# A decoder layer on one Trainium2 core: sums over tokens taken by GpSimd additions and one matmul, or by matmuls over four token tiles

## The chip, the cores and the metric

The kernel runs on one core of one Trainium2 chip, as one launch. The metric is the device time of the launch in microseconds (us), lower is better; the median of three runs is given with the lowest and the highest. Engines: TensorE (matmuls, PE in the profile, PEld its weight loads), VectorE (DVE), ScalarE (ACT), GpSimd (POOL) and SyncE (SP, which issues the DMAs here). Each engine works through its own queue in order and waits on semaphores that the others raise.

## The reference

16 batches of 512 tokens with 512 channels, fp32. Linear attention with 16 heads, then a cross attention over channels, then a mixture of experts with one expert of 8 per batch, each followed by a layer norm. Cut to what matters here:

```
x = layernorm(x + linear_attention(x))                 # x1
scores = einsum('bhdn,bhen->bhde', q, k) * scale       # q = x*wq + bq, k = ctx*wk + bk; sum over tokens n
x = layernorm(x + channel_attention(x, ctx))           # x2, global and local weights
top1 = argmax(einsum('bh,he->be', x.mean(axis=1), Wr) + br)   # the mean is over the 512 tokens
h = relu(x @ W1[top1] + b1[top1]); out = h @ W2[top1] + b2[top1]
x = layernorm(x + out)
```

Two sums over the 512 tokens of a batch stand in it: that of `x1` per channel, since the scores with q = x*wq + bq and the bias bk of the keys come apart into terms of which one is (sum of x1)*wq*bk, and that of `x2` per channel, for the router.

## The kernel before

`mixers` computes both attentions for all batches and stores `x2` in HBM; `experts` then does the experts, with products split into high and low parts. Tokens lie in four tiles of 128 (`TT = 4`), channels in four groups of 128 (`CC = XH = 4`).

`mixers` is a software pipeline over steps i = 0 to 18 (`staged`: three written out, steps 3 to 14 as a loop on each engine, four written out). In step i, batch a = i gets its keys, values and queries, b = i - 1 its denominator, projection and first layer norm, c = i - 2 its channel attention and second norm, e = i - 3 its router. So from step 3 to step 15 all four are there; step 16 has b, c and e, step 17 c and e, step 18 e alone. The order in each engine's queue is written out by hand.

TensorE's queue in a step: the k product of a (three fp32r matmuls for each of four channel groups, L868), the denominators of b (L918), v of a, the broadcast of the reciprocals (L933, L940) around q of a, then the two sums over tokens: `mean_ps` of e (L949) and `sx_ps` of c (L956), then k of a's group 1, the router's product (L968), v and q, k and v of group 2, two tiles of the projection, the transposes of the channel weights (L990), q of group 2, the channel attention's output (L1011), the rest of the projection, k, v, q of group 3, and last the sum of the context (L1030) and the raw scores (L1043) of b, which use `x1`.

For the sums, GpSimd adds the four token tiles of `x1` (b, `tile_sum(0, ...)`) and of `x2` (c, `tile_sum(1, ...)`) at the end of its step into `x_sum` (L292, L296), three instructions on 128x512 each. A step later TensorE multiplies each 128 channels of `x_sum` with a column block of ones (32 columns): four products for each sum, which the profile shows as eight instructions, since an fp32 product is two. ScalarE copies the results out as `m_col` (L451, for the router) and `s_x` (L458), in this order and after both sums, because they lie in one PSUM bank. Behind them in ScalarE's queue stands `y_hi` of channel groups 2 and 3 (L405), from which GpSimd makes `y_lo` (L308) and after it adds a bias to all of `x_tok` in one instruction on 128x2048 (L312).

VectorE's queue in a step: the inner score products (L646, L647), the denominator (L778 and on), keys and values of group 0 (L536, L547, two scans), `y` times its reciprocal (L763), the outer score products (L653, L657), query and numerator (L558, L566, L576), then `token_sums` (L622, L623, L626), which reads `s_x`, the rest of the scores up to their scaled maximum (L667 to L682), keys and values of group 1 and so on. At the end of the step stand `xT_lo` of the next batch (L749) and L558, L566, L576 of group 3.

GpSimd's addition of `const_b` to `x1` (L331) waits for its own `x1` sum (`xsum_done`), and VectorE's write of `x2` (L595) for that of the batch before (`x2sum_done`).

Of the kernel before, what the change touches and what calls it, by code (L numbers as in the profile page):

```python
# [11 lines left out]
P = 128  # L12
# [43 lines left out]
def mixers(nc, d, idx, x2_dram, x2_stored):  # L56

    with ExitStack() as ctx:
        def sb(name, shape, dt=F32):
            return ctx.enter_context(nc.sbuf_tensor(name, shape, dt))  # L60

        def sem(name):
            return ctx.enter_context(nc.semaphore(name))
# [57 lines left out]
        k_all, k_all2 = sb("k_all", [P, XH]), sb("k_all2", [P, XH])  # L121
        aT = sb("aT", [P, XH, P])
        const_b = sb("const_b", [P, C])
        x_sum = sb("x_sum", [P, 2, C])
        m_col = sb("m_col", [P, CC])
        logits = sb("logits", [1, NE])
        top = sb("top", [1, NE])
# [50 lines left out]
        mean_mm, mcol_done, route_mm, logit_done, top_done, idx_done = (  # L178
            sem(n) for n in ("mean_mm", "mcol_done", "route_mm", "logit_done", "top_done", "idx_done"))
        found_done = sem("found_done")  # L180
        xsum_done, x2sum_done = sem("xsum_done"), sem("x2sum_done")
        rall_done = sem("rall_done")

        block = ctx.enter_context(nc.Block())
# [55 lines left out]
        def _(pool):  # L240
# [41 lines left out]
                    pool.wait_ge(mr_done[n], due)  # L282
                pool.tensor_tensor(shift[:, n, :], m_r[:, n, :], minus[:, :], ALU.mult).then_inc(shift_done[n], 1)

            def tile_sum(n, b, x, x_done, used, done):

                if (due := upto(b, TT, TT)) is not None:
                    pool.wait_ge(x_done, due)

                if (due := upto(b - 1, 1, 1)) is not None:  # L290
                    pool.wait_ge(used, due)
                pool.tensor_tensor(x_sum[:, n, :], x[:, 0, :], x[:, 1, :], ALU.add).then_inc(done, 1)  # L292
                for t in range(2, TT):
                    if (due := upto(b, TT - 1, t - 1)) is not None:
                        pool.wait_ge(done, due)
                    pool.tensor_tensor(x_sum[:, n, :], x_sum[:, n, :], x[:, t, :], ALU.add).then_inc(done, 1)  # L296

            def step(i):
                b, c = i - 1, i - 2
                if inside(b):  # L300
# [13 lines left out]
                if inside(c):  # L314

                    if (due := upto(c, 1, 1)) is not None:
                        pool.wait_ge(kall2_done, due)

                    if (due := upto(c, 1, 1)) is not None:
                        pool.wait_ge(c_mm, due)  # L320
                    pool.tensor_tensor(diag[:, :, :], ident[:, :].unsqueeze(1).broadcast_to([P, XH, P]),
                                       k_all2[:, :].unsqueeze(2).broadcast_to([P, XH, P]), ALU.mult).then_inc(diag2_done, 1)
                    if (due := upto(c, 1, 1)) is not None:
                        pool.wait_ge(kb_done, due)

                    if (due := upto(c, 1, 1)) is not None:
                        pool.wait_ge(g_mm, due)
                    if (due := upto(c, TT - 1, TT - 1)) is not None:
                        pool.wait_ge(xsum_done, due)
                    for t in range(TT):  # L330
                        pool.tensor_tensor(x1[:, t, :], x1[:, t, :], const_b[:, :], ALU.add).then_inc(x1c_done, 1)  # L331
                if inside(b):
# [8 lines left out]
                    rstd_of(0, b)  # L341
                if inside(c):
                    rstd_of(1, c)
                if inside(b):
                    tile_sum(0, b, x1, x1_done, sx_mm, xsum_done)
                if inside(c):
                    tile_sum(1, c, x2, x2_done, mean_mm, x2sum_done)

            staged(pool, step)

# [164 lines left out]
        def _(dve):  # L515
# [62 lines left out]
            def residual(n, b, t):  # L578
                mm, res, done, src, dst = ((proj_mm, x_tok, res1_done, x_tok, x_tok),
                                           (out_mm, x1, res2_done, x1, x2))[n]  # L580
                if (due := upto(b, TT, t + 1)) is not None:
                    dve.wait_ge(mm, due)
                if n == 0:
                    if (due := upto(b, 1, 1)) is not None:
                        dve.wait_ge(xb_done, due)
                else:
                    if (due := upto(b, TT, t + 1)) is not None:
                        dve.wait_ge(x1c_done, due)

                    if (due := upto(b - 1, TT - 1, TT - 1)) is not None:  # L590
                        dve.wait_ge(x2sum_done, due)
                    if (due := upto(b - 1, 16, 16)) is not None:
                        dve.wait_ge(x2_stored, due)
                ps = WIDE[t % 2]
                dve.tensor_tensor(dst[:, t, :], ps[:, :], src[:, t, :], ALU.add).then_inc(done, 1)  # L595
# [265 lines left out]
        def _(pe):  # L861
# [34 lines left out]
            def step(i):  # L896
# [46 lines left out]
                        pe.wait_ge(den_max, due)  # L943
                if inside(e):

                    if (due := upto(e, TT - 1, TT - 1)) is not None:
                        pe.wait_ge(x2sum_done, due)
                    for j in range(CC):
                        last = pe.matmul(mean_ps[:, j, :], x_sum[:, 1, j * P:j * P + P], ones[:, 0:SUM], start=True, stop=True)  # L949
                    last.then_inc(mean_mm, 1)  # L950
                if inside(c):

                    if (due := upto(c, TT - 1, TT - 1)) is not None:
                        pe.wait_ge(xsum_done, due)
                    for h in range(XH):
                        last = pe.matmul(sx_ps[:, h, :], x_sum[:, 0, h * P:h * P + P], ones[:, 0:SUM], start=True, stop=True)  # L956
                    last.then_inc(sx_mm, 1)
                if inside(a):
                    qkv(a, 1, "k")
# [496 lines left out]
```

## Time and profile before

| | |
|---|---|
| runs | median 2728.85 us (2728.75 to 2729.05, 3 runs) |
| the profiled execution, its span | 2728.0 us |
| TensorE busy | 2471.1 us (91%) |
| VectorE busy | 1893.2 us (69%) |
| ScalarE busy | 994.4 us (36%) |
| GpSimd busy | 684.0 us (25%) |
| DMA | 97 GB/s in the mean, 264.09 MB |

The profile's own execution took its span and less than 1 us around it. `mixers` takes the first 1262 us of it, `experts` the rest. The page cuts the span into 40 slices of 68 us; in each row a digit is the busy share in tenths:

```profile
PE   7988888888889888854999999999999999999998
DVE  6899999999999999964455555555555455545553
POOL 3344444444454445442011001100111011101110
```

The reader sees two parts: in the first eighteen slices VectorE is at nine tenths and TensorE at eight, in the others TensorE alone is full. Times in rows are us from the start of the span; a row of the timeline has start, length, engine, line, operation, output<-inputs, shapes (partitions x elements) and number of instructions, and in brackets for how long the engine was idle before it and who ended that.

### The profile page before, as it was taken

The page shows a single profiled execution, that of the slowest core. Times are in us where ns is not written, and L with a number is a line of the kernel's source. Part 1 is how long each engine was busy: PE and PEld are TensorE (multiplying, and loading weights), DVE is VectorE, ACT ScalarE, POOL GpSimd, SP SyncE. Part 2 cuts the span into 40 slices and gives each one's busy share as a digit, 9 for nine tenths or more (in the row PEclk, how much of TensorE's full clock was granted, in tenths as well). Part 3 has the DMA queues.
Part 4 walks back from the last instruction along what each step waited for, and adds up shares of the span by engine and source line. Part 5 has one row for each costly group of instructions (what it writes and reads, how often), then busy time and mean ns, then how long its engine had stood idle before and what let it go on. Part 6 is the DMA issues. An engine that isn't in the chain of part 4 may idle for free.

```text
span 2728.0 us, 35480 instructions
## 1 busy us (share of the span) xinstructions
PE 2471.1 (91%) x11584; PEld 2008.6 (74%) x11584; DVE 1893.2 (69%) x2904; ACT 994.4 (36%) x1639; POOL 684.0 (25%) x521
## 2 busy tenths in 40 slices
PE   7988888888889888854999999999999999999998
PEld 5766666667667666743888887878878788888886
DVE  6899999999999999964455555555555455545553
ACT  4433433344434434322333333333333333333332
POOL 3344444444454445442011001100111011101110
PEclk9999999999999999976999999999999999999999
DMA  4121112112222221113333343324332433243321
GB/s 189 47 78 57 42 71 77 69 70 77 77 77 77 77 77 38 44 74 125 107 129 111 101 143 128 119 87 143 130 122 82 143 135 123 76 143 135 135 72 68
DMA packets 59002, 264.09 MB, mean 97 GB/s; under 512 B 9106, under 2 KB 9106, under 8 KB 43922
## 3 DMA queue, kind: packets, MB, share of 16 engines
q1 hardware_dynamic: 58898, 262.60, 26.8%
q8 instruction: 78, 1.28, 0.2%
q14 instruction: 26, 0.21, 0.0%
HBM read 229.02 MB, written 33.55 MB: 96 GB/s over the span
## 4 chain that ended last, share of the span: by engine, by line
PE 52%; issue 0%; DVE 0%; DMA 0%; ACT 0%; POOL 0%; ACTq 0%; POOLq 0%; DVEq 0%
PE h_ps L1358 26%; PE acc L1376 26%; PE t_ps L1336 1%; DMA x_res<-x_scratch 0%; DVE we_lo L1257 0%; ACT x_res L1242 0%; DVE stats_e L1310 0%; ACT x2T_hi L1213 0%; POOL rstd_f L1186 0%; ACT we_hi L1205 0%; ACTq L1056 0%; DVE x2T_lo L1264 0%; DVE mv_e L1321 0%; POOLq L1056 0%; POOL var_f L1183 0%
## 5 line engine op out<-in xcount | busy, mean ns | idle before, releaser
L1229 ACT ACTIVATE hid<-h_ps,b 128x512 f32<-128x512 f32 x256 | 176.1, 688 | 727.3 <-PE h_ps L1358 727.3
L1280 DVE CAST h_hi<-hid 128x512 fp32r<-128x512 f32 x256 | 113.5, 443 | 457.3 <-ACT hid L1229 457.3
L868 PE MATMUL bank<-xT_hi,w_hi 128*128 128x512 f32 x768 | 332.2, 433 | 106.1 <-DVE kv_sum L547 79.6
L1358 PE MATMUL h_ps<-x2T_hi,we_hi 128*128 128x512 f32 x1024 | 407.1, 398 | 15.6 <-issue 9.8
L1358 PE MATMUL h_ps<-x2T_lo,we_hi 128*128 128x512 f32 x1024 | 400.5, 391 | 0.0
L1358 PE MATMUL h_ps<-x2T_hi,we_lo 128*128 128x512 f32 x1024 | 400.5, 391 | 0.0
L1376 PE MATMUL acc<-we_hi,h_lo 128*128 128x512 f32 x1024 | 399.0, 390 | 0.0
L1376 PE MATMUL acc<-we_hi,h_hi 128*128 128x512 f32 x1024 | 398.8, 389 | 0.0
L1376 PE MATMUL acc<-we_lo,h_hi 128*128 128x512 f32 x1024 | 398.8, 389 | 0.0
L1257 DVE TENSOR_TENSOR we_lo<-raw,we_hi 128x1024 fp32r<-128x1024 f32 x256 | 314.6, 1230 | 107.4 <-ACT we_hi L1205 107.4
L1183 POOL TENSOR_TENSOR var_f<-mv_e,ln_eps_e 128x4 f32<-128x4 f32 x16 | 17.3, 1082 | 1328.1 <-DVE mv_e L1321 1328.1
L868 PE MATMUL bank<-xT_lo,w_hi 128*128 128x512 f32 x768 | 318.0, 414 | 0.0
L868 PE MATMUL bank<-xT_hi,w_lo 128*128 128x512 f32 x768 | 318.0, 414 | 0.0
L1205 ACT ACTIVATE we_hi<-raw 128x1024 fp32r<-128x1024 f32 x256 | 269.5, 1054 | 118.1 <-DMA raw<-in_w 118.1
L868 PEld LDWEIGHTS bank<-xT_hi,w_hi 128*128 128x128 f32 x768 | 153.5, 200 | 156.1 <-DVE kv_sum L547 86.2
L1283 DVE TENSOR_TENSOR h_lo<-hid,h_hi 128x512 fp32r<-128x512 f32 x256 | 237.8, 929 | 8.8
L1358 PEld LDWEIGHTS h_ps<-x2T_hi,we_hi 128*128 128x128 f32 x1024 | 193.1, 189 | 50.5 <-issue 12.2
L1358 PEld LDWEIGHTS h_ps<-x2T_lo,we_hi 128*128 128x128 f32 x1024 | 193.3, 189 | 44.9 <-issue 6.9
L1358 PEld LDWEIGHTS h_ps<-x2T_hi,we_lo 128*128 128x128 f32 x1024 | 193.0, 189 | 41.6
L1376 PEld LDWEIGHTS acc<-we_hi,h_hi 128*128 128x128 f32 x1024 | 192.4, 188 | 40.0
L1376 PEld LDWEIGHTS acc<-we_lo,h_hi 128*128 128x128 f32 x1024 | 192.3, 188 | 39.7
L1376 PEld LDWEIGHTS acc<-we_hi,h_lo 128*128 128x128 f32 x1024 | 192.3, 188 | 39.7
(147 smaller groups left out, 3968.3 us busy)
## 6 DMA issues: line engine op xcount, KB each, us to landing
raw<-in_w SPq DMA_DIRECT2D x256, 512.0 KB, 3.3
xT_raw<-in_xT SPq DMA_DIRECT2D x16, 1024.0 KB, 9.5
x_tok<-in_x_tok SPq DMA_DIRECT2D x16, 1024.0 KB, 6.7
ctx_tok<-in_ctx_tok SPq DMA_DIRECT2D x16, 1024.0 KB, 8.8
ctx_T<-in_ctxT SPq DMA_DIRECT2D x16, 1024.0 KB, 4.7
x_scratch<-x SPq DMA_DIRECT2D x16, 1024.0 KB, 4.8
x_res<-x_scratch SPq DMA_DIRECT2D x16, 1024.0 KB, 4.9
out_dram<-x_res SPq DMA_DIRECT2D x16, 1024.0 KB, 4.8
```

The costliest lines, as they stand in the source:

```text
L868: last = pe.matmul(out, lhsT, rhs, start=(n == 0), stop=(n == 3 * len(pairs) - 1))
L1183: pool.tensor_tensor(var_e[:, :], mv[:, :, 1], ln_eps[:, :], ALU.add).then_inc(ve_done, 1)
L1205: act.activation(w_hi[:, f % NW, :], raw[:, f % NR, :], ACT.Copy).then_inc(whi_done, 1)
L1229: act.activation(hid[:, f % 2, :], h_ps[f % 2][:, :], ACT.Relu, bias=b1[:, parity, f:f + 1]).then_inc(h_done, 1)
L1257: dve.tensor_tensor(w_lo[:, f % NW, :], raw[:, f % NR, :], w_hi[:, f % NW, :].bitcast(F32), ALU.subtract).then_inc(wlo_done, 1)
L1280: dve.tensor_copy(h_hi[:, s, :], hid[:, f % 2, :]).then_inc(hhi_done, 1)
L1283: dve.tensor_tensor(h_lo[:, s, :], hid[:, f % 2, :], h_hi[:, s, :].bitcast(F32), ALU.subtract).then_inc(hlo_done, 1)
L1336: last = pe.transpose(t_ps[j % 2][:, t * P:t * P + P], x_res[parity][:, t, j * P:j * P + P], ident[:, :])
L1358: last = pe.matmul(h_ps[f % 2][:, :], wx[:, s, js], xx[parity][:, j, :], start=(n == 0), stop=(n == 3 * CC - 1))
L1376: last = pe.matmul(acc[t][:, :], hx[:, s, ts], wx[:, sw, C:], start=(f == 0 and n == 0), stop=(f == FC - 1 and n == 2))
```

## The change

The additions on GpSimd, the buffer `x_sum` and the semaphores `xsum_done` and `x2sum_done` go. TensorE multiplies each of the four token tiles of `x1` and `x2` itself with the ones and lets PSUM accumulate them: 16 products for each sum where there were 4, so 64 instructions for 16 in a step that has both. It waits for the normalised tiles (`x1_done`, `x2_done`). GpSimd's L331 now waits for `sx_mm`, VectorE's L595 for `mean_mm`.

```diff
@@ mixers, GpSimd
-                    if (due := upto(c, TT - 1, TT - 1)) is not None:
-                        pool.wait_ge(xsum_done, due)
+                    if (due := upto(c, 1, 1)) is not None:
+                        pool.wait_ge(sx_mm, due)
                     for t in range(TT):
                         pool.tensor_tensor(x1[:, t, :], x1[:, t, :], const_b[:, :], ALU.add).then_inc(x1c_done, 1)
...
-                if inside(b):
-                    tile_sum(0, b, x1, x1_done, sx_mm, xsum_done)
-                if inside(c):
-                    tile_sum(1, c, x2, x2_done, mean_mm, x2sum_done)
@@ mixers, VectorE
-                    if (due := upto(b - 1, TT - 1, TT - 1)) is not None:
-                        dve.wait_ge(x2sum_done, due)
+                    if (due := upto(b - 1, 1, 1)) is not None:
+                        dve.wait_ge(mean_mm, due)
@@ mixers, TensorE
-                    if (due := upto(e, TT - 1, TT - 1)) is not None:
-                        pe.wait_ge(x2sum_done, due)
+                    if (due := upto(e, TT, TT)) is not None:
+                        pe.wait_ge(x2_done, due)
                     for j in range(CC):
-                        last = pe.matmul(mean_ps[:, j, :], x_sum[:, 1, j * P:j * P + P], ones[:, 0:SUM], start=True, stop=True)
+                        for t in range(TT):
+                            last = pe.matmul(mean_ps[:, j, :], x2[:, t, j * P:j * P + P], ones[:, 0:SUM],
+                                             start=(t == 0), stop=(t == TT - 1))
                     last.then_inc(mean_mm, 1)
                 if inside(c):
 
-                    if (due := upto(c, TT - 1, TT - 1)) is not None:
-                        pe.wait_ge(xsum_done, due)
+                    if (due := upto(c, TT, TT)) is not None:
+                        pe.wait_ge(x1_done, due)
                     for h in range(XH):
-                        last = pe.matmul(sx_ps[:, h, :], x_sum[:, 0, h * P:h * P + P], ones[:, 0:SUM], start=True, stop=True)
+                        for t in range(TT):
+                            last = pe.matmul(sx_ps[:, h, :], x1[:, t, h * P:h * P + P], ones[:, 0:SUM],
+                                             start=(t == 0), stop=(t == TT - 1))
                     last.then_inc(sx_mm, 1)
```

## Rows read from the trace of the kernel before

**Rows 1.** Stretch, us, busy of PE, PEld, DVE, ACT, POOL (count), PEclk, DMA, GB/s.
```profile
191.80:1087.90 896.10, 765.94 (x3889) 609.96 (x3889) 836.57 (x1405) 360.92 (x745) 416.50 (x301) 0.95 0.18 70
```
**Rows 2.** Timeline of TensorE: one looped step, then parts of later steps.
```profile
640.15 2.43 PE L918 MATMUL bank<-qk,head_sum 128*32 128x128 f32 x32 [0.42 <-DVE qk L566]
...
645.18 0.40 PE L868 MATMUL bank<-xT_hi,w_lo 128*128 128x512 f32 x1
...
652.74 0.98 PE L949 MATMUL bank<-ones,x_sum 128*128 128x32 f32 x8
653.55 1.06 PE L956 MATMUL bank<-ones,x_sum 128*128 128x32 f32 x8
654.45 0.48 PE L868 MATMUL bank<-xT_hi,w_hi 128*128 128x512 f32 x1
...
670.77 0.80 PE L868 MATMUL bank<-xT_hi,w_hi 128*128 128x512 f32 x1 [4.40 <-DVE kv_sum L547]
...
711.34 0.49 PE L868 MATMUL bank<-xT_hi,w_hi 128*128 128x512 f32 x1 [0.70 <-DVE xT_lo L749]
...
725.88 0.97 PE L949 MATMUL bank<-ones,x_sum 128*128 128x32 f32 x8
...
1084.54 0.47 PE L868 MATMUL bank<-xT_hi,w_hi 128*128 128x512 f32 x1 [0.56 <-issue]
```
**Rows 3.** Timeline of ScalarE in the same step.
```profile
654.90 0.17 ACT L458 ACTIVATE s_x<-bank 128x4 f32<-128x4 f32 x1
```
**Rows 4.** Timeline of VectorE in the same step.
```profile
643.80 0.28 DVE L778 TENSOR_SCALAR den<-bank 128x128 f32<-128x128 f32 x1
...
646.42 0.75 DVE L547 SCALAR_TENSOR_TENSOR kv_sum<-bank,b_qkv,k_sum 128x512 f32<-128x512 f32 x1
...
660.40 4.57 DVE L622 TENSOR_TENSOR s_q<-s_x,cols 128x4 f32<-128x4 f32 x1
...
668.88 0.29 DVE L682 TENSOR_SCALAR neg_scaled<-neg_max 128x4 f32<-128x4 f32 x2
...
675.64 0.69 DVE L558 SCALAR_TENSOR_TENSOR q<-e_q,r_q 128x512 f32<-128x512 f32 x1
...
707.40 3.70 DVE L749 TENSOR_TENSOR xT_lo<-xT_raw,xT_hi 128x1024 fp32r<-128x1024 f32 x2 [0.82 <-ACT xT_hi L382]
711.02 1.77 DVE L558 SCALAR_TENSOR_TENSOR q<-e_q,r_q 128x512 f32<-128x512 f32 x1
```
**Rows 5.** Timeline of VectorE in step 16.
```profile
1172.68 0.15 DVE L622 TENSOR_TENSOR s_q<-s_x,cols 128x4 f32<-128x4 f32 x1
...
1183.22 0.28 DVE L682 TENSOR_SCALAR neg_scaled<-neg_max 128x4 f32<-128x4 f32 x2
```
**Rows 6.** Timeline of GpSimd in the looped step.
```profile
659.89 5.05 POOL L312 TENSOR_TENSOR x_tok<-x_tok,rows 128x2048 f32<-128x2048 f32 x1
...
707.88 4.36 POOL L296 TENSOR_TENSOR x_sum<-x_sum,x 128x512 f32<-128x512 f32 x2
```
**Rows 7.** Timeline of TensorE in steps 16, 17 and 18.
```profile
1167.65 1.75 PE L949 MATMUL bank<-ones,x_sum 128*128 128x32 f32 x8
1169.21 1.90 PE L956 MATMUL bank<-ones,x_sum 128*128 128x32 f32 x8
...
1221.66 1.58 PE L949 MATMUL bank<-ones,x_sum 128*128 128x32 f32 x8 [1.77 <-POOL x_sum L296]
...
1259.06 1.91 PE L949 MATMUL bank<-ones,x_sum 128*128 128x32 f32 x8 [12.87 <-POOL x_sum L296]
```
**Rows 8.** Short stretches in steps 16 and 17, columns as in rows 1.
```profile
1167.50:1170.80 3.30, 3.30 (x17) 3.21 (x16) 3.30 (x3) 0.17 (x1) 2.91 (x2) 0.50 0.01 5
1171.70:1175.40 3.70, 0.25 (x8) 0.13 (x6) 3.63 (x6) 1.23 (x2) 2.50 (x3) 0.50 0.01 2
1213.70:1218.00 4.30, 4.29 (x20) 4.29 (x21) 0.00 (x0) 2.78 (x4) 4.11 (x4) 0.50 0.17 72
1218.00:1219.90 1.90, 1.89 (x14) 1.69 (x13) 0.00 (x0) 0.00 (x0) 1.82 (x2) 0.83 0.94 388
```

More of the change, by code:

```diff
@@ L123, in mixers @@
         const_b = sb("const_b", [P, C])
-        x_sum = sb("x_sum", [P, 2, C])
         m_col = sb("m_col", [P, CC])
@@ L180, in mixers @@
         found_done = sem("found_done")
-        xsum_done, x2sum_done = sem("xsum_done"), sem("x2sum_done")
         rall_done = sem("rall_done")
@@ L283, in rstd_of @@
                 pool.tensor_tensor(shift[:, n, :], m_r[:, n, :], minus[:, :], ALU.mult).then_inc(shift_done[n], 1)
[L285 to L296, printed above, removed]
             def step(i):
```

## The prediction

> **What bounds the kernel now.** I read the engines' busy times over the twelve looped steps of the mixer first, then one step of it on TensorE, ScalarE, VectorE and GpSimd in order of time, and last the granted clock. The twelve steps last 896.1 us, so one lasts 74.7 us; VectorE is busy for 836.57 us of them (93%), TensorE for 765.94 (85%), GpSimd for 416.50 (46%) [rows 1]. So a step goes at VectorE's pace, with TensorE close behind: TensorE waits 4.40 us for VectorE's `kv_sum` of L547 before its product at 670.77 and 0.70 us for `xT_lo` at 711.34 [rows 2]. Work added to TensorE ahead of the 4.40 us wait could vanish in it. The question is who waits for the sums themselves. ScalarE reads them out (L458) at 654.90 [rows 3]; VectorE comes to that result only at 660.40, at L622, 5.3 us after it is there [rows 4]. That slack of 5.3 us is what the added work has to fit into.
>
> The same VectorE rows hold the other side. L622 is an operation on 128x4 and takes 4.57 us there, and 0.15 us at 1172.68 [rows 4, 5]; meanwhile GpSimd runs its one 128x2048 addition of 5.05 us [rows 6]. A 128x512 operation with two SBUF operands (L558) takes 0.69 us at 675.64 and 1.77 us at 711.02, where GpSimd is in the `x_sum` additions of L296, 4.36 us for two [rows 4, 6]. So an operation of VectorE that meets one of GpSimd waits until that one ends. Taking the sums from GpSimd gives VectorE time back.
>
> The expert part (from about 1262 us on) has none of the changed lines and I cost it at nothing.
>
> **GpSimd's additions leave.** Each is three instructions per batch. In a looped step they lie beside the end of VectorE's step: the two `xT_lo` at 707.40 and the three operations L558, L566 and L576 behind them. One of the three costs 1.77 - 0.69 = 1.08 us too much [rows 4], so the three 3.2 us, besides what `xT_lo` gains. But that is not what the step gains. Next late is TensorE's den product (L918), for which VectorE's L778 waits. It now ends at 640.15 + 2.43 = 642.58 and L778 starts at 643.80 [rows 2, 4]. TensorE itself gets earlier only by its two waits on VectorE: 0.42 us before L918, and of the 0.70 us before the first product 0.14 us, since the entry into a step costs 0.56 us even where nothing is waited for (1084.54) [rows 2]. So den ends at 642.02, and L778 gains 1.8 us, not 3.2. Then L547 needs the v product, which ends at 645.18 + 0.40 - 0.56 = 645.02: L547 starts there instead of at 646.42, and 1.4 us are left of the gain [rows 2, 4]. Beyond this the old queue order holds: GpSimd's `const_b` addition, `y_lo` and the 128x2048 addition stay and go on meeting VectorE.
>
> **TensorE's sums grow.** 16 matmul instructions per step (each fp32 product is two) become 64. At full clock 16 take 654.45 - 652.74 = 1.71 us, 0.107 us each [rows 2]. At half clock eight take 1169.21 - 1167.65 = 1.56 us, 0.195 each, and the next eight 1.90 us [rows 7], 0.24 each; I take 0.20, near the start to start value, since the 1.90 hold the end of the last one too. So 64 take 6.8 us at 2.4 GHz and 12.8 us at 1.2 GHz.
>
> Which clock? From 1167.50 to 1170.80 TensorE did nothing but these sums, busy all 3.30 us, at a granted clock of 0.50, and at 1171.70 to 1175.40 it is still 0.50. From 1213.70 to 1218.00 it did the products of L1043 at 0.50, and from 1218.00 on the row's mean is 0.83, so it had risen [rows 8]. So the sums did not lift the clock and the products of L1043 did. I take from it that the sums do not hold it either, and that it falls during the 6.8 us. No row shows that directly; today's sums last 1.7 us. I put the fall in the middle: 32 at 0.107 and 32 at 0.20 make 9.8 us. Bounds: after a quarter of them 1.7 + 9.6 = 11.3 us, after three quarters 5.1 + 3.2 = 8.3 us.
>
> **One looped step.** Where the clock did not fall before them, the sums start at 725.88, that is 651.2 in the step I use. Their start hangs on VectorE's `y` (L763), so it moves with VectorE, to 651.2 - 1.4 = 649.8. They end 9.8 us later, at 659.6. From their end to the `s_x` result are 654.90 + 0.17 - 654.45 = 0.62 us [rows 2, 3], so L622 can start at 660.2. VectorE would be there at 660.40 - 1.4 - 2 x 1.0 = 657.0 (L566 and L576 ahead of L622 are free of `y_lo`, which now comes later, because ScalarE has the copies L451 and L458 ahead of `y_hi` of chunks 2 and 3 in its queue, and GpSimd takes `y_lo` from there). So VectorE waits 3.2 us for the sums: a new wait, and behind it in VectorE's queue stand the score operations, on which ScalarE's exponentials wait. The relief from the 128x2048 addition doesn't come either: `y_lo` and it are held up by the same wait and now meet the operations behind L622. A row shows that alignment: in step 16 L622 starts at 1172.68 and L682 ends at 1183.50, 10.8 us [rows 5]. So L682 ends at 660.2 + 10.8 = 671.0, against 668.88 + 0.29 = 669.17 now [rows 4]: 1.9 us later per step. Bounds from 8.3 and 11.3 us of sums: 0.4 to 3.4 us. TensorE's own 8.1 us more (9.8 for 1.7) meet a start 2.9 us earlier than 652.74 and the wait of 4.40 us at 670.77, and VectorE's `kv_sum`, 1.9 us later, still comes last there, so nothing is added for TensorE. Thirteen steps (3 to 15) have both sums with all the rest: 13 x 1.9 = 24.7 us, bounds 5 and 44. Step 2 has one sum only, 32 instructions or 1.7 us more inside 5.3 us of slack: nothing.
>
> **The last three steps**, without attention products, where TensorE is cold. Step 16: 48 more at 0.20 are 9.6 us, less the 1.2 us by which VectorE comes later than `s_x` today (sums end 1169.21 + 1.90, L622 starts 1172.68, 0.4 us lie between) and 1.0 us of relief ahead: 7.4 us. Step 17: today TensorE idles 1.77 us for GpSimd at 1221.66 [rows 7]; that goes, the first 16 or so run in it at full clock (1.5 us saved), 9.6 - 1.8 - 1.5 = 6.3 us. Step 18: the GpSimd additions of 4 us ahead of 1259.06 go, 24 more at 0.20 come: 0.8 us. Sum 14.5 us, bounds 8 (step 16 warm) and 17.
>
> **Sum.** 2728.0 + 24.7 + 14.5 = 2767.2 us span. The runs' median is 2728.85, 0.8 us more than the profiled span, so 2768 us.
>
> **Two rules of the skill.** The Trainium skill, SBUF — State Buffer, "SBUF: two separate sides", says that GpSimd and VectorE share one port pair as an exclusive lock and that the loser is blocked for the whole instruction. The rows of 4.57 us agree. Taken alone it speaks for a gain, which is rival B. The Trainium skill, TensorE: Matmul & The Clock Gate, "What's actually happening", says that activity releases the throttle; if weight loads and short matmuls back to back are activity, the clock holds: rival A.
>
> **The rivals.** The forecast: the clock falls within the sums and VectorE waits for them. Chance 0.66.
> A: the clock holds in the loop. For it: the sums keep TensorE busy without a gap, and in the rows at 725.88 they run at 0.107. Against it: the 3.30 us at 0.50. Sums of 6.8 us end at 656.6, L622 at 657.3, L682 ends at 668.1: 1.1 us per step gained, 13 x 1.1 = 14 us, against 14.5 us lost at the end: 2729 us. Chance 0.15.
> B, the other side: the clock holds and GpSimd's 128x2048 addition meets the reductions of L678 (a single operand, 1.3 us for two) in place of two-operand work. Then 1.1 + 1.2 = 2.3 us per step are gained, 30 us, less 14.5: 2713 us. It decides itself at L622: the sums must be read before VectorE gets there. Chance 0.10.
> C: the clock falls early and stays at half through the products behind the sums. Eleven of these take 645.18 - 642.58 = 2.6 us at full clock, so 24 at half clock cost up to 5.7 us more; with 9.6 us of added sums (11.3 for 1.7) that is 15.3 us, less the 2.9 and 4.40 us of before and 2.8 us that the twelve products at 670.77 gain if the clock is up there: TensorE becomes the bound, by about 5 us per step, 65 + 17 = 82: 2811 us. For it: nothing in the sums lifts the clock. Chance 0.09.
>
> **How the numbers follow.** Range: A lies at its lower end, the forecast's upper bound (44 + 17) at 2790; 2727 to 2790 leaves out B and C, 0.19. About 0.2%, 5.5 us, is what a measurement of this kernel can tell from no change. Faster: B, 0.10. Same: A, 0.15, and a thin edge of the forecast, 0.01. Slower: the rest, 0.74.
>
> **What would show it.** Right: the granted clock falls to 0.50 within the 64 sums (L949 and L956 now); VectorE idle before L622, released by ScalarE's `s_x`; L558, L566, L576 at the end of a step at 0.69 us; no wait at `xT_lo` before the first product; a step of 76 to 77 us; L622 in step 16 about 7 us later against its step's start. Wrong: a granted clock of 1.00 throughout the sums (A), a step below 74 us (B), or the longest wait of TensorE gone and VectorE waiting for products of L868 (C).

## The result, and the profile after

The kernel with TensorE's sums takes 2743.45 us in the median (2740.08 to 2748.45, four runs), the kernel before in the same comparison 2728.8 us (2728.09 to 2729.05, four runs). The ratio is 1.0059, 95% interval 1.0044 to 1.0073: 0.6% slower. 2768 us was forecast, so the direction was right, the range (2727 to 2790) holds the time, and the loss was forecast at 2.7 times its size. The profiled execution is the fastest of the four, 2740.08 us, with a span of 2738.3 us; all accounts below go from span to span, 2728.0 to 2738.3, which is 10.3 us. The medians are 14.7 us apart; the other 4.3 us are the distance of the fastest run of the kernel after from its median, and only the fastest was profiled.

The page of the kernel after, engines' busy time, share and instructions:

```profile
span 2738.3 us, 36806 instructions
PE 2588.5 (95%) x12352; PEld 2128.4 (78%) x12352; DVE 1829.8 (67%) x2904; ACT 993.5 (36%) x1639; POOL 527.3 (19%) x425
```

TensorE has 768 instructions and 117 us of busy time more, VectorE 63 us less although it executes the same instructions, GpSimd 157 us less. The twelve looped steps, with the columns of [rows 1]:

```profile
194.60:1096.60 902.00, 854.98 (x4464) 700.22 (x4464) 782.07 (x1405) 360.06 (x744) 294.62 (x228) 0.93 0.18 70
```

A step lasts 75.2 us where it lasted 74.7. VectorE falls from 836.57 to 782.07 us of work, which is 4.5 us per step, and the step is still longer: its time is now in waits. One looped step on TensorE, to set beside [rows 2] (its first product is the one at 636.91, not shown, without any idle time before it):

```profile
646.09 0.72 PE L914 MATMUL bank<-rden_all,head_all 128*128 128x512 f32 x2 [0.74 <-ACT rden_all L415]
...
650.09 3.65 PE L931 MATMUL bank<-ones,x 128*128 128x32 f32 x32
653.57 5.57 PE L940 MATMUL bank<-ones,x 128*128 128x32 f32 x32
658.96 0.77 PE L849 MATMUL bank<-xT_hi,w_hi 128*128 128x512 f32 x1
```

The first 32 instructions last 3.48 us from start to start (0.109 each), the next 32 5.39 us: the sums together 8.87 us. Stretches of the same time, with us, TensorE's busy time and count, granted clock, DMA share and GB/s, then the sums of step 16:

```profile
650.10:655.00 4.90, 4.90 (x46) 1.00 0.11 45
655.00:656.00 1.00, 1.00 (x8) 0.58 0.00 0
656.00:662.00 6.00, 6.00 (x22) 0.50 0.00 0
662.00:668.00 6.00, 6.00 (x33) 1.00 0.00 0
1171.20:1178.00 6.80, 6.80 (x34) 0.50 0.12 48
1178.00:1184.90 6.90, 6.88 (x33) 0.50 0.00 0
```

The clock falls from 2.4 to 1.2 GHz within the sums, after 46 of the 64 instructions, although TensorE is busy without a gap; it stays low behind them and is back at 662. In step 16 it was low before and the sums pass at half clock throughout, 13.8 us. VectorE and ScalarE in the looped step:

```profile
633.91 2.36 DVE L730 TENSOR_TENSOR xT_lo<-xT_raw,xT_hi 128x1024 fp32r<-128x1024 f32 x2 [0.82 <-ACT xT_hi L363]
636.19 0.69 DVE L539 SCALAR_TENSOR_TENSOR q<-e_q,r_q 128x512 f32<-128x512 f32 x1
...
642.50 0.29 DVE L759 TENSOR_SCALAR den<-bank 128x128 f32<-128x128 f32 x1 [1.90 <-PE bank L899]
...
659.64 0.17 DVE L603 TENSOR_TENSOR s_q<-s_x,cols 128x4 f32<-128x4 f32 x1 [2.27 <-ACT s_x L439]
...
660.11 2.37 DVE L648 TENSOR_TENSOR a_v<-rows,s_q 128x512 f32<-128x512 f32 x2
662.40 6.79 DVE L655 TENSOR_TENSOR s_a<-s_a,a_v 128x512 f32<-128x512 f32 x2
...
670.30 0.28 DVE L663 TENSOR_SCALAR neg_scaled<-neg_max 128x4 f32<-128x4 f32 x2
```

```profile
659.43 0.17 ACT L439 ACTIVATE s_x<-bank 128x4 f32<-128x4 f32 x1
```

```profile
663.59 5.05 POOL L297 TENSOR_TENSOR x_tok<-x_tok,rows 128x2048 f32<-128x2048 f32 x1
```

Against [rows 4]: the two `xT_lo` last 2.36 us where they lasted 3.70, and L539 (L558 before) 0.69 where it was 1.77, which is the relief. VectorE then waits 1.90 us for the denominators, and 2.27 us at L603 (L622 before), released by ScalarE's copy of the sums: the new wait. And L655 (L674 before) takes 6.79 us for two instructions, because GpSimd's 5.05 us addition [rows 6] now lies beside it and no more beside L622.

### The profile page after: what moved, and what is told of

The parts are those of the page before. It is cut to its first block, busy times and chain, and to the rows that moved or that the text cites. A ratio compares the mean times of both kernels' runs of the same rounds, so it can differ in the third digit from the quotient of the medians.

```text
span 2738.3 us, 36806 instructions
## 1 busy us (share of the span) xinstructions
PE 2588.5 (95%) x12352; PEld 2128.4 (78%) x12352; DVE 1829.8 (67%) x2904; ACT 993.5 (36%) x1639; POOL 527.3 (19%) x425
## 4 chain that ended last, share of the span: by engine, by line
PE 52%; DVE 0%; issue 0%; DMA 0%; ACT 0%; POOL 0%; ACTq 0%; POOLq 0%; DVEq 0%
PE h_ps L1343 26%; PE acc L1361 25%; PE t_ps L1321 1%; DMA x_res<-x_scratch 0%; DVE we_lo L1242 0%; ACT x_res L1227 0%; DVE stats_e L1295 0%; ACT x2T_hi L1198 0%; POOL rstd_f L1171 0%; ACT we_hi L1190 0%; ACTq L1041 0%; DVE x2T_lo L1249 0%; DVE mv_e L1306 0%; POOLq L1041 0%; POOL var_f L1168 0%
```

## Where the 10.3 us come from

I cut both traces at the same instructions: the first of the products that broadcast the reciprocals (L933 before, L914 after) in steps 3 and 16, the transposes of the channel weights in step 16, and the first product of the experts.

| stretch | before | after | difference | forecast |
|---|---|---|---|---|
| start to step 3 | 199.06 | 194.62 | -4.4 | 0 |
| steps 3 to 15 (13) | 965.83 | 974.09 | +8.3 | +24.7 |
| step 16 to the first expert product | 113.32 | 126.76 | +13.4 | +14.5 |
| `experts` | 1449.8 | 1442.9 | -6.9 | 0 |
| sum | 2728.0 | 2738.3 | +10.3 (rounded parts: 10.4) | +39.2 |

The last row of the table is a surprise: the change touches nothing in `experts`. TensorE's costliest group in that part, of the kernel before and of the kernel after (line, engine, operation, shapes and count, then busy us and mean ns, then the idle time before its instructions and by whom ended):

```profile
L1358 PE MATMUL h_ps<-x2T_hi,we_hi 128*128 128x512 f32 x1024 | 407.1, 398 | 15.6 <-issue 9.8 <-DVE we_lo L1257 5.8
```

```profile
L1343 PE MATMUL h_ps<-x2T_hi,we_hi 128*128 128x512 f32 x1024 | 406.6, 397 | 9.7 <-DVE we_lo L1242 5.8 <-issue 3.9
```

"issue" is time in which TensorE waited for nothing that the profile shows. It was 9.8 us and is 3.9 us. It stands at fixed places of the loop over the batches (one turn does two of them), two per turn before and one after:

```profile
1637.72 0.49 PE L1358 MATMUL h_ps<-x2T_hi,we_hi 128*128 128x512 f32 x1 [0.72 <-issue]
...
1640.91 0.39 PE L1358 MATMUL h_ps<-x2T_hi,we_hi 128*128 128x512 f32 x1 [1.55 <-issue]
```

```profile
1655.14 0.49 PE L1343 MATMUL h_ps<-x2T_hi,we_hi 128*128 128x512 f32 x1 [1.05 <-issue]
...
1834.17 0.49 PE L1343 MATMUL h_ps<-x2T_hi,we_hi 128*128 128x512 f32 x1 [0.68 <-issue]
```

## The experiments

The theory is the forecast's: relief of VectorE, sums in which the clock falls, a wait for them. Rivals: that relief and sums are worth something else than each was put at and meet by chance; that the loss is the order of the queues and not the clock; and, for `experts`, that the gain comes from some other state of the chip and not from the code. Times are medians, ratios against the kernel before in the same comparison, with 95% intervals.

**The relief alone.** GpSimd's additions are gone as in the change, TensorE does no more products than before.

```diff
@@ mixers, TensorE, against the kernel after; the other sum alike
-                        for t in range(TT):
-                            last = pe.matmul(sx_ps[:, h, :], x1[:, t, h * P:h * P + P], ones[:, 0:SUM],
-                                             start=(t == 0), stop=(t == TT - 1))
+                        last = pe.matmul(sx_ps[:, h, :], x1[:, 0, h * P:h * P + P], ones[:, 0:SUM], start=True, stop=True)
```

> Leaves out work: TensorE sums token tile 0 alone (4 products a sum, as in the kernel before), GpSimd adds nothing; so the two sums are those of a quarter of the tokens. It shows what GpSimd's additions cost alone. Theory (VectorE is freed of them, but TensorE's den product is next late): a looped step of 72.5 us (74.7 before), no wait of VectorE before its use of s_x, time 2690 to 2705. Rival (the whole 4.4 us of VectorE's time comes back): a step of 70.3 us, 2675. Rival (VectorE is not what sets the step): a step of 74.7 us, 2728.

Measured: 2692.7 us, ratio 0.9869 (0.9852 to 0.9885), a looped step 72.38 us. The relief is worth 2.29 us per step. This is inside what was expected, and VectorE has no wait at L603. L603 takes 4.56 us there, as before the change: beyond the two `xT_lo` and the operations behind them, GpSimd and VectorE go on meeting as the forecast said.

```profile
632.96 0.97 PE L930 MATMUL bank<-ones,x 128*128 128x32 f32 x8
633.77 1.06 PE L937 MATMUL bank<-ones,x 128*128 128x32 f32 x8
...
642.28 4.56 DVE L603 TENSOR_TENSOR s_q<-s_x,cols 128x4 f32<-128x4 f32 x1
```

**The sums alone.** GpSimd adds as before, each of TensorE's products for the sums is done four times.

```diff
@@ mixers, TensorE, against the kernel before; the other sum alike
                     for h in range(XH):
-                        last = pe.matmul(sx_ps[:, h, :], x_sum[:, 0, h * P:h * P + P], ones[:, 0:SUM], start=True, stop=True)
+                        for t in range(TT):
+                            last = pe.matmul(sx_ps[:, h, :], x_sum[:, 0, h * P:h * P + P], ones[:, 0:SUM], start=True, stop=True)
```

> The kernel before with its GpSimd additions, but TensorE does each product of the sums four times (same result). It shows the 64 instructions alone. Theory (the clock falls in the sums and VectorE waits for them): granted clock 0.50 from about 5 us into the sums, VectorE idle before L622 for 0.5 to 1.5 us, a looped step of 76.5 to 77.5 us, time 2760 to 2775. Rival (the sums fit into the slack of 5.3 us and TensorE's wait of 4.4 us): a step of 74.7 us and only the last three steps longer, 2740.

Measured: 2786.8 us, ratio 1.0214 (1.0194 to 1.0233), a looped step 77.62 us; both are above what was expected. The longer sums cost 2.95 us per step. The wait stands at the place that was named and is longer than the 0.5 to 1.5 us that were expected:

```profile
666.64 3.65 PE L950 MATMUL bank<-ones,x_sum 128*128 128x32 f32 x32
670.13 5.57 PE L958 MATMUL bank<-ones,x_sum 128*128 128x32 f32 x32
...
676.19 0.16 DVE L622 TENSOR_TENSOR s_q<-s_x,cols 128x4 f32<-128x4 f32 x1 [2.34 <-ACT s_x L458]
```

-2.29 and +2.95 make +0.66 us per step; the whole change measures +0.50 (75.17 less 74.67, the mean of twelve steps). The two parts nearly add up. So the small net loss is a difference of two large terms, 30 us and 38 us over thirteen steps.

**A wider product with the ones.** The same 64 instructions with the same weights, but 128 columns of ones in place of 32, so TensorE streams four times as much. The results need more of PSUM than is free in the old bank, so each sum goes to one of the two banks of the scores, with four more waits on three semaphores; `SUM` is the number of columns.

```diff
@@ against the kernel after
-SUM = 32
+SUM = 128
...
-        sx_ps, mean_ps = (DEN_BANK[:, n:n + XH * SUM].rearrange("p (h e) -> p h e", h=XH) for n in (P, P + XH * SUM))
+        sx_ps, mean_ps = (b[:, :].rearrange("p (h e) -> p h e", h=XH) for b in (G_BANK, C_BANK))
```

> The changed kernel with one size changed: the moving operand of the sums is 128 columns of ones instead of 32, with the same number of instructions and the same weights; the results go to the two banks of the scores, which are free then. Theory (the sums let the clock fall because they stream little): granted clock 1.00 through the sums of a looped step, which last 7.1 us instead of 9, VectorE waits 0.5 us instead of 2.3, a step of 73.5 us (75.2 in the changed kernel), and steps 16 to 18 shorter by 2 to 5 us: time 2715 to 2725. Rival (wider products cost more time than the clock gives): sums of 9 us or more, 2743 or above. Rival (the clock falls for another reason, the weight loads): clock 0.50 as before, 2743 to 2750.

Measured: 2706.07 us, ratio 0.9919 (0.9902 to 0.9935), a looped step 72.90 us, which is faster than was expected. The timeline around the sums, then their stretch (columns as above):

```profile
635.49 3.77 PE L935 MATMUL bank<-ones,x 128*128 128x128 f32 x32
639.10 3.74 PE L948 MATMUL bank<-ones,x 128*128 128x128 f32 x32
...
643.33 0.16 DVE L603 TENSOR_TENSOR s_q<-s_x,cols 128x4 f32<-128x4 f32 x1 [0.55 <-ACT s_x L439]
```

```profile
635.50:642.60 7.10, 7.10 (x66) 1.00 0.09 38
```

The granted clock is 1.00 from the first to the last, the sums last 7.11 us where they lasted 8.87, VectorE waits 0.55 us where it waited 2.27. The kernel does more work per sum and is 37 us faster than the one with 32 columns, faster even than the kernel before (8 us of that lie in `experts`, see below). The forecast's mechanism is seen here from its other side: the clock held, and the wait shrank with it. That it is the number of columns that lets the clock fall or holds it is the plain reading, but the banks and the four waits were changed with the columns, and no run puts 32 columns into the new banks, so this one step isn't shown apart from them. In step 16, where the clock is low as the sums begin, the 128 columns bring it up:

```profile
1141.50:1144.50 3.00, 3.00 (x15) 0.50 0.22 90
1144.50:1147.00 2.50, 2.50 (x21) 0.81 0.00 0
1147.00:1150.70 3.70, 3.70 (x34) 1.00 0.00 0
```

The 64 instructions there last 9.2 us (1141.54 to about 1150.7); those with 32 columns stayed at 0.50 for all of their 13.8 us.

**The router's sum moved back in the queue.** Nothing needs `mean_ps` soon, VectorE needs `sx_ps`. TensorE's sum for the router goes behind k of group 2, ScalarE's copy of it and the router's product behind that.

```diff
@@ mixers, TensorE, against the kernel after
-                if inside(e):
-
-                    if (due := upto(e, TT, TT)) is not None:
-                        pe.wait_ge(x2_done, due)
-                    for j in range(CC):
-                        for t in range(TT):
-                            last = pe.matmul(mean_ps[:, j, :], x2[:, t, j * P:j * P + P], ones[:, 0:SUM],
-                                             start=(t == 0), stop=(t == TT - 1))
-                    last.then_inc(mean_mm, 1)
...
+                    qkv(a, 2, "k")
                 if inside(e):
...
+                    for j in range(CC):
+                        for t in range(TT):
+                            last = pe.matmul(mean_ps[:, j, :], x2[:, t, j * P:j * P + P], ones[:, 0:SUM],
+                                             start=(t == 0), stop=(t == TT - 1))
+                    last.then_inc(mean_mm, 1)
```

> The changed kernel with the router's sum moved: TensorE does it behind the k product of group 2, where it waited 4.4 us in the kernel before, and the router's product and ScalarE's copy follow it; only the 32 instructions of the scores' sum stay where they were. Theory (VectorE's wait for s_x is what the change costs in a looped step): no wait of VectorE at s_x, a step of 72.5 to 73 us, steps 16 to 18 about 6 us longer than before instead of 13, time 2695 to 2712. Rival (TensorE's own added work is the bound): VectorE waits elsewhere for TensorE's products, a step of 75 us, 2735 to 2745.

Measured: 2690.17 us, ratio 0.9861 (0.9844 to 0.9877), a looped step 72.19 us: the fastest of all kernels here, together with the one below, and faster than was expected. In the step shown each sum alone passes at full clock:

```profile
632.16 3.65 PE L927 MATMUL bank<-ones,x 128*128 128x32 f32 x32
...
641.45 4.57 DVE L599 TENSOR_TENSOR s_q<-s_x,cols 128x4 f32<-128x4 f32 x1
...
646.93 3.65 PE L944 MATMUL bank<-ones,x 128*128 128x32 f32 x32
```

```profile
632.10:635.60 3.50, 3.50 (x33) 1.00 0.17 70
646.90:650.40 3.50, 3.50 (x33) 1.00 0.00 0
```

That isn't so in every step: of the thirteen sums for the scores in steps 3 to 15 three lasted 4.2 to 4.5 us, at a mean granted clock of 0.82 (487.40 to 491.70), 0.81 (921.00 to 925.30) and 0.76 (1064.60 to 1069.20). VectorE has no wait for `s_x` in any of the thirteen, and the step (72.19 us) is that of the relief alone (72.38 us): the sums have become free in the loop. They aren't free behind it: from step 16 to the first expert product it takes 116.7 us, 109.4 in the relief alone. The work is that of the change, only the order differs. The rival that it is the order is therefore right too, for a different part of the same wait: 64 instructions back to back are long at full clock (7.11 us with 128 columns), and they are slower still at half.

**Both of these.**

```diff
@@ against the kernel with the router's sum moved back
-SUM = 32
+SUM = 128
```

> The router's sum moved as in router_later, and the sums with 128 columns of ones as in cols128. Theory (two separate costs: VectorE's wait in the looped step, which the move alone removes, and cold sums in steps 16 to 18, which 128 columns shorten): looped step as router_later, 72.2 us, from the last broadcast of step 16 to the first expert product 2 to 5 us less than its 116.7 us, time 2684 to 2689. Rival (the bank of const_b, now written by the router's sum, makes a new wait): 2690 or more.

Measured: 2690.78 us, ratio 0.9862 (0.9846 to 0.9878), a looped step 72.05 us. No difference from the one above. From step 16 to the first expert product it takes 118.2 us against 116.7, which is not the shortening that was expected: a stall of TensorE with the releaser "issue", 2.62 us, stands before the sums of step 17.

**The scores' sum on TensorE, the router's with GpSimd.**

```diff
@@ mixers, TensorE, against the kernel before
-                    if (due := upto(c, TT - 1, TT - 1)) is not None:
-                        pe.wait_ge(xsum_done, due)
+                    if (due := upto(c, TT, TT)) is not None:
+                        pe.wait_ge(x1_done, due)
                     for h in range(XH):
-                        last = pe.matmul(sx_ps[:, h, :], x_sum[:, 0, h * P:h * P + P], ones[:, 0:SUM], start=True, stop=True)
+                        for t in range(TT):
+                            last = pe.matmul(sx_ps[:, h, :], x1[:, t, h * P:h * P + P], ones[:, 0:SUM],
+                                             start=(t == 0), stop=(t == TT - 1))
...
@@ mixers, GpSimd
-                if inside(b):
-                    tile_sum(0, b, x1, x1_done, sx_mm, xsum_done)
```

> One part of the change alone: the sum of x1 for the scores is accumulated by TensorE, that of x2 for the router stays with GpSimd's additions. 40 instructions of sums in a step, 4.3 us. Theory (VectorE's wait at s_x is the price, its meetings with GpSimd the gain): the sums end before VectorE comes, no wait at s_x, but x2's three additions still meet VectorE at the end of its step: 72.5 to 73.5 us a step, time 2705 to 2720. Rival (any accumulation on TensorE costs): 2730 or more.

Measured: 2694.24 us, ratio 0.9876 (0.9859 to 0.9892), a looped step 72.31 us, faster than was expected. With the additions of `x2` left on GpSimd the step keeps all of the relief (72.31 against 72.38): taking away those of `x1` is enough. The trace shows why those of `x2` cost nothing there. Without the others ahead of it VectorE is further on, and they lie beside its products of scores, which read a PSUM bank and go on at 0.68 us each, and beside its wait for the denominators; in the kernel before they reached into L566 and L576, 1.67 and 1.75 us each:

```profile
692.82 0.68 DVE L645 TENSOR_TENSOR a_v<-bank,cols 128x512 f32<-128x512 f32 x1
...
693.15 1.29 POOL L292 TENSOR_TENSOR x_sum<-x 128x512 f32<-128x512 f32 x1 [5.98 <-ACT x L391]
...
693.42 0.68 DVE L644 TENSOR_TENSOR s_a<-bank,cols 128x512 f32<-128x512 f32 x1
```

The opposite split, `x1` with GpSimd and `x2` on TensorE, was not run. The 40 instructions of both sums lasted 4.4 to 6.0 us in the looped steps, so here too the clock fell in some, and VectorE had no wait for `s_x` in any of them.

**Moving TensorE's code.** The change adds, by my count, 480 instructions to TensorE's program: the sums are written at ten places, each gets twelve more products, and a product is four instructions (the profile shows two loads and two matmuls for an fp32 product). The kernel before, with waits that are met at once put at the head of TensorE's program, moves the code of `experts` without touching it:

```diff
@@ mixers, TensorE, against the kernel before
         def _(pe):
+            for _ in range(480):
+                pe.wait_ge(xT_in, 16)
```

> The kernel before with 480 waits that are already met at the start of TensorE's queue, as many instructions as the change adds to TensorE's code. Nothing else differs, so it shows what the place of the expert loop's code costs. Theory (the second stall in each turn of TensorE's expert loop, 0.9 to 1.6 us with no releaser, comes from where its code lies): from the first expert product to the end 1443 us as in the changed kernel (1449.8 before), one such stall a turn in place of two; the start is 0 to 15 us later for the waits themselves. Rival (the shorter expert part comes from the state in which mixers leaves the engines): 1449.8 us and two stalls.

Measured: 2739.96 us, ratio 1.0041 (1.0027 to 1.0055); the waits themselves delay the start by 19 us. As was expected, from the first expert product (1297.41) to the end it takes 1443.0 us: the figure of the kernel after (1442.9), not that of before (1449.8). The same group as above:

```profile
L1360 PE MATMUL h_ps<-x2T_hi,we_hi 128*128 128x512 f32 x1024 | 406.6, 397 | 9.9 <-DVE we_lo L1259 5.8 <-issue 4.1
```

This was tried at other distances: 32 waits in the kernel after, then 32 and 224 in the kernel before, with the same edit.

> The changed kernel with 32 waits that are already met at the start of TensorE's queue: with the 480 instructions of the change that makes 512. Theory (place of the code, repeating every 128, 256 or 512 instructions): the second stall in a turn of the expert loop is back, 1449 to 1450 us from the first expert product to the end in place of 1442.9. Rival (state of the engines, or another period): 1443 us.

> The kernel before with 32 met waits at the start of TensorE's queue; only the place of its code changes. Theory (the two stalls in a turn of the expert loop hang on where its code lies, finer than 480 instructions): one stall a turn and 1443 us from the first expert product to the end. Rival (only a large shift matters): two stalls and 1449.8 us.

> As before_pad32 with 224 waits, which is 480 less 256. Theory (a period of 256 instructions or a divisor of it): as with 480 waits, one stall a turn and 1443 us. Rival (no period there): 1449.8 us.

Measured, with the time from the first expert product to the end:

| kernel | whole | first expert product | `experts` | "issue" in that group |
|---|---|---|---|---|
| before | 2728.8 | 1278.21 | 1449.8 | 9.8 |
| before, 32 waits (one run, before 2728.22) | 2745.68 | 1277.20 | 1466.7 | 19.4 |
| before, 224 waits (one run, before 2728.22) | 2724.14 | 1281.47 | 1440.9 | 2.5 |
| before, 480 waits | 2739.96 | 1297.41 | 1443.0 | 4.1 |
| after | 2743.45 | 1295.47 | 1442.9 | 3.9 |
| after, 32 waits | 2743.7 | 1303.44 | 1443.0 | 3.7 |

Places and "issue" are those of the profiled run, which for the kernel after with 32 waits is the slowest of its four, 2748.13 us; that kernel has a ratio of 1.0053 (1.0037 to 1.007). Only the runs with 480 and with 224 waits came out near what was expected; the two with 32 waits didn't (1466.7 where 1443 was expected, and 1443.0 where 1449 to 1450 was). With 32 waits in the kernel before each turn of the loop has one long stall:

```profile
1640.07 0.49 PE L1360 MATMUL h_ps<-x2T_hi,we_hi 128*128 128x512 f32 x1 [3.91 <-issue]
...
1823.85 0.79 PE L1360 MATMUL h_ps<-x2T_hi,we_hi 128*128 128x512 f32 x1 [3.83 <-issue]
```

So where TensorE's instructions of that loop lie makes 26 us of difference (1440.9 to 1466.7, single runs) without one instruction of the loop changed, and 32 instructions ahead of it, which cost nothing themselves, cost 17 us. 9.6 of these are longer "issue"; with them comes the clock, which is at half behind four of the five long stalls, as in the row here, and was at 1.00 at this place in the kernel before:

```profile
1642.00:1644.00 2.00, 2.00 (x6) 0.50 0.00 0
```

The idea behind the run of the kernel after with 32 waits, that the pattern repeats with 512 instructions so that 480 and 32 make a whole turn, fell: it stayed at 1443.0. The other kernels fit: the relief alone, with as many TensorE instructions as before, has 1449.8 us in `experts` like the kernel before (2691.5 - 1241.71); the sums alone, with the 480 more, 1442.0 (2783.0 - 1341.01). It matters for the ratios above: `experts` takes 1441.8 us with 128 columns, 1442.6 with the router's sum moved back and 1442.9 with the scores' sum alone on TensorE. So 7 to 8 us of what these kernels gain over the kernel before come from the place of the code and not from what was changed in `mixers`, and the relief alone is the fastest of all up to the first expert product (1241.71, against 1246.34 with the router's sum moved back and 1278.21 before).

## Why the prediction was right in its mechanism and wrong in its size

The mechanism came as forecast, the size didn't: 39.2 us were forecast and 10.3 came. The term that failed is the relief of VectorE. It put the start of the sums 1.4 us earlier; they start 2.3 us earlier, because the 0.56 us that the forecast left as the price of entering a step were a wait for `xT_lo` like the others and went too. `experts` at nothing (6.9 us) and the length of the sums (5.5 us) come next.

**Which resource it is about: right.** VectorE paces the step, and the sums are on the path through `s_x` and not through TensorE's time. The wait at L603 stands in each looped step, 1.4 to 4.2 us; 3.2 were forecast.

**The clock falls within the sums: right, and nearly at the place.** 46 of 64 instructions passed first in the step shown, where the middle was taken. The sums last 8.87 us there and 9.38 us in the mean of steps 3 to 15, for 9.8; the thirteen lie between 8.04 (step 3) and 10.80, all but the first within the bounds of 8.3 and 11.3. The middle was a choice between two bounds and read off no row, so that it came this close is in part luck. In the sum this is 0.42 us per step too much, 5.5 us in thirteen.

**The relief of VectorE: right in kind, too small in size.** This is the step that failed most. I let TensorE's first product gain 0.14 of its 0.70 us wait, because the entry into step 15 (the first one written out behind the loop) shows 0.56 us of "issue" [rows 2], and I took that for the price of any entry. It isn't one. In the kernel before, `xT_lo` of that step ends at 1080.74 + 3.70 = 1084.44, and the product starts at 1084.54:

```profile
1080.74 3.70 DVE L749 TENSOR_TENSOR xT_lo<-xT_raw,xT_hi 128x1024 fp32r<-128x1024 f32 x2 [0.81 <-ACT xT_hi L382]
```

By these rows the 0.56 us were a wait for VectorE's `xT_lo` that the profile gave no releaser, and this `xT_lo` was one of those that GpSimd stretched (3.70 us, 2.36 without it). The kernels that keep the additions of `x1` on GpSimd all show the 0.56 us at this place, with waits put ahead of their code or not (before, with 32, 224 and 480 waits, and the sums alone); none of the others does. In the kernel after, neither the first product of step 15 nor that of the step shown has idle time before it. So the whole 0.70 us went. The denominators' L759 starts 9.94 us behind the step's anchor (the first product of the context's sum) where its like started 12.43 us behind it: 2.49 us gained for 1.8. The sums start 17.53 us behind the anchor, 18.42 by the forecast: 0.9 us per step, 11.6 us in thirteen. 0.56 of the 0.9 is this misread wait. The rest lies at the same two waits: the first product starts 3.49 us behind the products before it (633.42 to 636.91) where it started 4.43 us behind them (632.23 to 636.66), which is 0.94 less and not 0.70, and the product for the denominators gains 0.51 and not 0.42. A product that waits for nothing starts a little before the profile's end of the one ahead of it, so more than the idle time goes.

**The operations behind `s_x` meet GpSimd: right.** From the start of L603 to the end of L663 it takes 670.58 - 659.64 = 10.94 us; 10.8 were read off step 16. So 1.9 - 0.9 - 0.4 + 0.1 = 0.7 us per step remain of the forecast's 1.9, and 8.3 / 13 = 0.64 were measured.

**The first steps: wrong.** Step 2 was costed at nothing because its one sum fits into the slack. It does; but the additions of these steps no longer meet VectorE either (step 2 lasts 72.04 us for 74.54), and the start to step 3 is 4.4 us shorter. The `xT_lo` of step 2 lasted 4.44 us and lasts 2.36; behind it 1.44 us of TensorE's "issue" at 115.73 are gone, which were a wait for it in the same way (it ended at 115.63). The edit was costed, its relief wasn't.

**The last three steps: right in the sum (13.4 for 14.5), off in the parts.** To the transposes of step 16 it takes 35.9 us for 27.1: +8.8, where 7.4 were forecast. From there to those of step 17 it takes 49.5 for 46.2: +3.3, where 6.3 were, since the first of its sums passed at full clock and the second at a mean of 0.79 (below), where 16 at full clock and the rest at half were assumed. Step 18: +1.4 for 0.8. The sum is right because these errors cancel.

```profile
1232.70:1236.20 3.50, 3.50 (x34) 1.00 0.02 7
1236.20:1240.80 4.60, 4.60 (x34) 0.79 0.00 0
```

**`experts` at nothing: wrong, -6.9 us.** It has none of the changed lines, but it lies behind them in TensorE's program, and the run with 480 waits shows that this place alone gives the 6.9 us. What was missing wasn't a term that rows of before could size: they show the 9.8 us of "issue", and not what a shift makes of it.

Together: 16.4 us of the 28.9 us between forecast and result lie in the loop (11.6 the earlier start of the sums, 5.5 their length, -1.8 the 10.94 us for 10.8, and 1.1 from rounding the terms and reading one step for all), 6.9 us in `experts`, 4.4 us in the first steps, 1.1 us in the last.

**The rivals.** A, the clock holds, and C, it stays low so long that TensorE becomes the bound, didn't come: the granted clock tells. What A described has a kernel of its own, that with 128 columns, and A's price was too high: it gave 2729 us, the run gave 2706, of which the relief counted too small and `experts` counted at nothing (8 us there) are the larger part. What rival B expected, GpSimd's 128x2048 addition beside the reductions of L678, came in none of the steps 3 to 15: it lies beside L655 in the kernel after and in that with 128 columns, and beside L603 or its like (4.56 us) in the relief alone and with the router's sum moved back.

What is open: by which rule the place of TensorE's instructions makes its loop stall, which the four distances don't settle; whether the number of columns alone holds the clock, without the change of banks; whether GpSimd's sums in the last three steps alone would take the 13 us there away; and whether the router's sum moved back and a better place of `experts` add up. The last three were not tried.

## What to carry to other kernels

Before work is moved to an engine, ask of each piece who waits for it: here one of the two sums is urgent and the other isn't, and the same change is 0.6% slower with the urgent one behind the other and 1.4% faster with the other moved back (both with 7 us, 0.3%, in favour of the change that are only the place of the code). Look at the granted clock within any added run of short matmuls, not only at their busy time; a wider moving operand can be cheaper than a narrow one. Where the profile names no releaser for a wait, look for an instruction that ends just before the wait does, before taking it for a fixed cost. And compare the parts of the two traces that the change doesn't touch, since a shift of code by itself moved `experts` here by -9 to +17 us.

## What the runs showed of the hardware that I had not expected

TensorE busy without a gap lost its clock: 46 fp32 instructions with 32 moving columns at 1.00, then 0.58 and 0.50, all at 100% busy. The same number of instructions with 128 columns (into other banks) kept 1.00 for their whole 7.11 us, raised it from 0.50 in step 16, and at full clock cost hardly more (0.111 us each against 0.109).

A loop of matmuls can stall at fixed places by where its code lies: 2.5 to 19.4 us of "issue" over `experts`, in single stalls of 0.5 to 4.0 us; a turn is two batches.

The kernel after spreads over 8.4 us in four runs, the one with 128 columns over 0.3 us, and the one with the sums alone, whose clock falls as well, over 9.8 us. The length of the sums in the kernel after also changes from step to step (8.04 to 10.80 us). I take from it that the moment at which the clock falls isn't fixed to the program; that was not tested further.
